# Routed experts of an attention + MoE kernel: second choices written plainly to first-choice slots, then added once into the output

## Time and profile before

| | value |
|---|---|
| median of three runs | 1812.68 us |
| the profiled execution | 1811.71 us, its span 1809.8 us |
| mean granted TensorE clock | 0.932 of full speed |
| PE / DVE / ACT / POOL busy | 82% / 69% / 43% / 71% of the span |
| chunk loop | from about 94 to 1196 us |
| first and last add into `out` (L466) | 1246.0 us and 1801.3 us; 288 instructions |

### The profile page before, as it was taken

One profiled execution on the slowest core, in us unless ns is written; L12 is line 12 of the kernel. 1 busy time (PEld: TensorE's weight loads), 2 busy tenths in 40 slices (PEclk: granted clock), 3 DMA queues, 4 the chain that ended last, 5 costly groups with the idle time before them and its releaser, 6 DMA issues.

```text
span 1809.8 us, 49252 instructions
## 1 busy us (share of the span) xinstructions
PE 1490.7 (82%) x17109; PEld 1315.5 (73%) x17110; DVE 1250.5 (69%) x3232; ACT 774.2 (43%) x1490; POOL 1276.1 (71%) x975
## 2 busy tenths in 40 slices
PE   5499999999999999999999999979776676676660
PEld 4477888888888888888888887758666665666650
DVE  7588888888888788888888887876434444334440
ACT  3244445445444444454455444425433333333330
POOL 5266666767676667666766766557888888888887
PEclk9699999999999999999999999999888889888885
DMA  8788888999898889888989988738777776777773
GB/s 195 136 212 184 171 174 209 197 178 192 209 183 179 192 194 188 180 192 211 180 174 210 201 174 185 178 137 213 136 130 134 134 133 108 132 132 134 134 113 36
DMA packets 929510, 302.36 MB, mean 167 GB/s; under 512 B 820882, under 2 KB 891160, under 8 KB 924480
## 3 DMA queue, kind: packets, MB, share of 16 engines
q1 hardware_dynamic: 859920, 178.50, 51.3%
q0 software_dynamic: 54432, 71.81, 21.7%
q10 hardware_dynamic: 15120, 51.57, 8.3%
HBM read 162.62 MB, written 143.43 MB: 169 GB/s over the span
## 4 chain that ended last, share of the span: by engine, by line
PE 38%; POOL 22%; issue 17%; DVE 14%; ACT 4%; SPq 2%; DMA 2%; POOLq 1%; DVEq 0%; ACTq 0%
POOL out L466 18%; ACT xn L568 3%; PE bank_a L1134 3%; PE bank_z L1119 3%; PE bank_y L1119 3%; PE bank_y L1121 3%; PE bank_y L1120 3%; PE bank_a L1273 3%; PE bank_z L1121 3%; PE bank_z L1120 3%; DVE ln_stats L879 2%; PE bank_a L1119 2%; PE bank_a L1121 2%; PE bank_a L1120 2%; PE bank_u L1119 2%
## 5 line engine op out<-in xcount | busy, mean ns | idle before, releaser
L466 POOL DMA_INDIRECT out<-v_area,tail x288 | 467.4, 1623 | 94.4 <-issue 89.1
L369 POOL DMA_INDIRECT slots<-xn,slot_i x256 | 263.8, 1031 | 134.5 <-DVE xn L830 71.7
L1119 PE MATMUL bank_y<-w_hi,xn_hi 128*128 x288 | 100.6, 349 | 148.8 <-DVE v_area L1075 81.7
L670 ACT ACTIVATE v_area<-bank_y,tail 128x256 f32<-128x256 f32 x144 | 60.5, 471 | 318.0 <-DVE tail L1067 314.1
L391 POOL TENSOR_TENSOR hid_lo<-hid,hid_hi 128x512 fp32r<-128x512 f32 x128 | 173.4, 1365 | 25.1 <-ACT hid_hi L539 23.6
L1119 PEld LDWEIGHTS bank_y<-w_hi,xn_hi 128*128 128x128 f32 x288 | 65.5, 228 | 163.9 <-issue 163.9
L1067 DVE COPY tail<-k_area 128x8 f32<-128x8 f32 x72 | 12.6, 175 | 245.7 <-DMA out<-v_area,tail 245.7
L539 ACT ACTIVATE hid_hi<-hid 128x512 fp32r<-128x512 f32 x128 | 80.6, 630 | 210.5 <-DVE hid L845 141.4
L1119 PE MATMUL bank_y<-wsh_out_hi,hid_hi 128*128 128x256 f32 x512 | 142.2, 278 | 0.0
L1120 PE MATMUL bank_y<-wsh_out_lo,hid_hi 128*128 128x256 f32 x512 | 141.9, 277 | 0.0
L1121 PE MATMUL bank_y<-wsh_out_hi,hid_lo 128*128 128x256 f32 x512 | 141.8, 277 | 0.0
(11 more groups left out here) (217 smaller groups left out, 4987.5 us busy)
## 6 DMA issues: line engine op xcount, KB each, us to landing
k_area<-slots SPq DMA_DIRECT2D x288, 129.0 KB
kv_dram<-w_sb SPq DMA_DIRECT2D x32, 1024.0 KB
x_sb<-in_x_in SPq DMA_DIRECT2D x32, 512.0 KB, 5.1
ctx_sb<-in_ctx_t SPq DMA_DIRECT2D x32, 512.0 KB, 5.0
q_dram<-q_sb SPq DMA_DIRECT2D x32, 512.0 KB
k_area<-kv_dram SPq DMA_DIRECT2D x256, 64.0 KB
w_sb<-q_dram SPq DMA_DIRECT2D x256, 64.0 KB
v_area<-kv_dram SPq DMA_DIRECT2D x256, 64.0 KB, 5.3
```

The lines of the kernel that those rows point to most:

```text
L369: pool.indirect_dma_start(slots[j], bass.IndirectOffsetOnAxis(ap=slot_i[:, j, i:i + 1], axis=0), row_of[j][:, i, :], None).then_inc(S[f"sc ...
L466: pool.indirect_dma_start(out, bass.IndirectOffsetOnAxis(ap=tail[:, r, t, 1 - j:2 - j].bitcast(u32), axis=0), y_ring[:, r, t, :], None, bo ...
L670: st = nc.scalar.activation(y_ring[:, r, t, :], Y[0][:, t * C:(t + 1) * C], ACT.Copy, scale=tail[:, r, t, j:j + 1])
L1119: mm(out, lhs_hi, rhs_hi, start=start, stop=False)
```

## The change

The roles are exchanged: the variable `FIRST = 1` names the table of the tokens' second choices, which is worked on in quads 0 to 35, and `SECOND = 0` that of the first choices, quads 36 to 71. Below, "first half" is quads 0 to 35 and "second half" quads 36 to 71.

- A row of a second choice no longer carries the token's number, but the row of the same token in the first choices' table (`SLOT_0`). In the first half POOL writes the weighted expert rows there, into a new table `sums`, with a plain indirect DMA (`ALU.bypass`). In the second half SP loads, beside the tiles, four tiles of `sums` into `y_ring` (`load_sums`), `expert_y` adds them, and POOL adds the result into `out`. Each token's row of `out` is thus added to once instead of twice.
- `expert_y` is DVE's alone, for all four tiles, and tells POOL after each two (`y_ready`). PE waits for both before its next `expert_down`.
- `pads(0)` also pads `sums` (six DMAs instead of three), comes before POOL's half of the `w2_lo` split instead of after it, and DVE waits for these pads before its half, since `pad` now lies where `y_ring` does.
- In the chunk loop the four steps of the shared block have four places (`hid_of`; two of them in `x_ring_t`), so that `shared_u` waits only for the chunk before. `x_round` and `x_split` of a chunk come one stage earlier (ACT between the copies of the turned tiles and their rounding, POOL ahead of `xn2_split`), `base_sum` writes to a buffer of its own, the scatters are in another order and their indices have two buffers.

```diff
+FIRST, SECOND = 1, 0
...
+        sums = nc.dram_tensor("sums", [NO_TILE + P, C], f32).ap()
...
-        pad = v_flat[:, 5632:5632 + PAD * ROW].rearrange("p (s f) -> p s f", s=PAD)
+        base = v_flat[:, 5120:5120 + BPC * C].rearrange("p (i f) -> p i f", i=BPC)
+        hid_of = [hid[:, 0, :], hid[:, 1, :]] + [x_ring_t[:, 2 * s:2 * s + 2, :].rearrange("p t f -> p (t f)") for s in range(2)]
+        pad_flat = v_flat[:, 0:PAD * ROW]
+        pad = pad_flat.rearrange("p (s f) -> p s f", s=PAD)
...
+            def load_x(j, n, r, at_rows, first):
+                if not first:
...
+                    sp.wait_ge(S["tail_ready"], at(1, n - 4, 1))
...
+                for t in range(4):
+                    sp.dma_start(x_ring[:, r, t, :], slots[j][bass.ds(at_rows[t], P), :]).then_inc(S[f"loaded{r}"], 16)
...
+            def load_sums(n, r, at_rows, first):
+                if not first:
+                    sp.wait_ge(S[f"added{r}"], at(16, n - r, 0))
+                for t in range(4):
+                    sp.dma_start(y_ring[:, r, t, :], sums[bass.ds(at_rows[t], P), :]).then_inc(S[f"held{r}"], 16)
...
+            sp.wait_ge(S["no_tile_stored"], 16 * (TOP + 1))
+            sp.wait_ge(S["padded1"], 16 * 3)
+            sp.wait_ge(S["scattered1"], 16 * BPC * CHUNKS)
+            first_rows = [tile_rows(q, q) for q in range(4)]
             for q in range(4):
-                load_quad(0, q, q, True, row_regs)
+                load_x(FIRST, q, q, first_rows[q], True)
             with sp.Fori(4, QUADS - 3, 4) as q:
                 for r in range(4):
-                    load_quad(0, q + r, r, False, row_regs)
...
+                    at_rows = tile_rows(q + r, r)
+                    load_x(FIRST, q + r, r, at_rows, False)
+            sp.wait_ge(S["scattered0"], 16 * BPC * CHUNKS)
+            sp.wait_ge(S["padded0"], 2 * 16 * 3)
+            second_rows = [tile_rows(QUADS + r, r) for r in range(4)]
+            for r in range(4):
+                load_x(SECOND, QUADS + r, r, second_rows[r], False)
+            for r in range(4):
+                sp.wait_ge(S[f"added{r}"], 16 * QUADS)
+            for r in range(4):
+                load_sums(QUADS + r, r, second_rows[r], True)
+            with sp.Fori(QUADS + 4, TOP * QUADS - 3, 4) as q:
                 for r in range(4):
-                    load_quad(1, q + r, r, False, row_regs)
+                    at_rows = tile_rows(q + r, r)
+                    load_x(SECOND, q + r, r, at_rows, False)
+                    load_sums(q + r, r, at_rows, False)
...
+            SCATTERS = [(j, i) for j in (FIRST, SECOND) for i in range(BPC)]
...
-                    nc.gpsimd.tensor_tensor(hid_lo[:, s, :], hid[:, s % 2, :], hid_hi[:, s, :], ALU.subtract).then_inc(S["hid_split"], 1)
+                    nc.gpsimd.tensor_tensor(hid_lo[:, s, :], hid_of[s], hid_hi[:, s, :], ALU.subtract).then_inc(S["hid_split"], 1)
...
+            def body(c, par, ahead_2):
                 xn2_split(c - 1)
-                if ahead:
-                    x_split(c + 1)
                 scale_probs(c)
-                scatter(c - 1, SCATTERS[:5])
-                hid_split(c - 1, range(2))
-                scatter(c - 1, SCATTERS[5:6])
+                scatter(c - 1, 1 - par, SCATTERS[:4])
+                hid_split(c - 1, range(1))
+                scatter(c - 1, 1 - par, SCATTERS[4:5])
+                hid_split(c - 1, range(1, 2))
+                scatter(c - 1, 1 - par, SCATTERS[5:6])
                 hid_split(c - 1, range(2, 3))
-                scatter(c - 1, SCATTERS[6:])
+                scatter(c - 1, 1 - par, SCATTERS[6:])
                 hid_split(c - 1, range(3, SB))
                 ln2_power(c)
                 if ahead_2:
                     ln1_power(c + 2, False)
                     ctx_split(c + 2)
-            with pool.Fori(1, CHUNKS - 2) as c:
-                body(c, True, True)
-            body(CHUNKS - 2, True, False)
-            body(CHUNKS - 1, False, False)
+                    x_split(c + 2)
...
+                for rows, width in ((slots[j], ROW), (sums, C))[:1 if j == FIRST else 2]:
+                    blocks = rows.rearrange("(b s) f -> b (s f)", s=PAD)
+                    for g in range(3):
+                        pool.indirect_dma_start(blocks if g else rows,
+                                                bass.IndirectOffsetOnAxis(ap=pad_at_i[:, j * 3 + g:j * 3 + g + 1], axis=0),
+                                                pad_flat[:, 0:PAD * width] if g else pad_flat[:, 0:width], None,
+                                                bounds_check=(NO_TILE + P) // (PAD if g else 1) - 1, oob_is_err=False).then_inc(S[f"padded{j}"], 16)
...
             xn2_split(CHUNKS - 1)
-            scatter(CHUNKS - 1, SCATTERS[:BPC])
+            scatter(CHUNKS - 1, 1, SCATTERS[:BPC])
             hid_split(CHUNKS - 1, range(1))
             pool.wait_ge(S["pad_at_ready"], 1)
             pool.wait_ge(S["pad_ready"], 1)
+            pads(1)
+            hid_split(CHUNKS - 1, range(1, SB))
+            scatter(CHUNKS - 1, 1, SCATTERS[BPC:])
             pads(0)
-            hid_split(CHUNKS - 1, range(1, SB))
-            scatter(CHUNKS - 1, SCATTERS[BPC:])
             pool.wait_ge(S["w2_hi_ready"], 1)
             pool.wait_ge(S["u_full"], SB * CHUNKS)
             half = slice(0, E * C // 2)
             nc.gpsimd.tensor_tensor(w2_lo[:, half], w2_sb[:, half], w2_hi[:, half], ALU.subtract).then_inc(S["w2_split"], 1)
-            pads(1)
-            def add(j, q, r):
-                n = j * QUADS + q
-                pool.wait_ge(S["ey_act"], at(1, n, 1))
-                pool.wait_ge(S["ey_dve"], at(1, n, 1))
-                pool.sem_inc(S["add_marked"], 1)
+            def pass_on(n, j, r):
+                target, last = (out, TOKENS - 1) if j == SECOND else (sums, NO_TILE + P - 1)
                 for t in range(4):
-                    pool.indirect_dma_start(out, bass.IndirectOffsetOnAxis(ap=tail[:, r, t, 1 - j:2 - j].bitcast(u32), axis=0),
-                                            y_ring[:, r, t, :], None, bounds_check=TOKENS - 1, oob_is_err=False,
-                                            compute_op=ALU.add).then_inc(S[f"added{r}"], 16)
-            pool.wait_ge(S["base_stored"], 16 * CHUNKS)
-            for q in range(4):
-                add(0, q, q)
-            with pool.Fori(4, QUADS - 3, 4) as q:
-                for r in range(4):
-                    add(0, q + r, r)
-            for r in range(4):
-                pool.wait_ge(S[f"added{r}"], 16 * QUADS)
+                    if t % 2 == 0:
+                        pool.wait_ge(S["y_ready"], at(2, n, t // 2 + 1))
+                        pool.sem_inc(S["add_marked"], 1)
+                    pool.indirect_dma_start(target, bass.IndirectOffsetOnAxis(ap=tail[:, r, t, 1 - j:2 - j].bitcast(u32), axis=0),
+                                            y_ring[:, r, t, :], None, bounds_check=last, oob_is_err=False,
+                                            compute_op=ALU.add if j == SECOND else ALU.bypass).then_inc(S[f"added{r}"], 16)
             with pool.Fori(0, QUADS - 3, 4) as q:
                 for r in range(4):
-                    add(1, q + r, r)
+                    pass_on(q + r, FIRST, r)
+            pool.wait_ge(S["base_stored"], 16 * CHUNKS)
+            with pool.Fori(QUADS, TOP * QUADS - 3, 4) as q:
+                for r in range(4):
+                    pass_on(q + r, SECOND, r)
...
-            def turned_out(c):
+            def turned_out(c, ahead_2):
                 for k in range(KT):
                     act.wait_ge(S["t2_full"], at(KT, c, k + 1))
                     nc.scalar.activation(xn2_t[:, k, :], XN2T_BANKS[k][:, :], ACT.Copy).then_inc(S["t2_out"], 1)
+                if ahead_2:
+                    x_round(c + 2)
...
-                    act.wait_ge(S["hid_split"], at(SB, c - 1, SB))
+                    act.wait_ge(S["hid_split"], at(SB, c - 1, 2))
                     load_x_t(c + 2)
...
-            def expert_y(n, j, r, first):
-                act.wait_ge(S["ey_full"], at(2, n, 1))
-                act.wait_ge(S["tail_ready"], at(1, n, 1))
-                if not first:
-                    act.wait_ge(S[f"added{r}"], at(16, n - r, 0))
-                for t in range(2):
-                    st = nc.scalar.activation(y_ring[:, r, t, :], Y[0][:, t * C:(t + 1) * C], ACT.Copy, scale=tail[:, r, t, j:j + 1])
-                st.then_inc(S["ey_act"], 1)
...
-                for j in range(TOP):
-                    st = nc.vector.tensor_copy(xn2[:, :, (1, 2 + C)[j]].bitcast(u32), row_id[:, :])
-                st.then_inc(S["row_step"], 1)
...
+                nc.vector.tensor_tensor(xn2[:, :, SLOT_0].bitcast(u32), slot_up[:, 0:BPC], slot_back[:, 0:BPC], ALU.add)
...
-                if s >= 2:
-                    dve.wait_ge(S["hid_split"], at(SB, c, s - 1))
-                nc.vector.scalar_tensor_tensor(out=hid[:, s % 2, :], in0=th[:, s % 2, :], scalar=0.5,
```

(30 more changed lines are left out.)

145 lines of the change are left out of this document (64 added, 81 removed).

## The result

The changed kernel takes 1841.3 us (median of four, 1836.9 to 1848.0) against 1814.1 us for the kernel before, timed beside it: a ratio of 1.015, 95% interval 1.010 to 1.019. Forecast were 1743 us with a range of 1716 to 1780. The profiled execution took 1842.6 us with a span of 1840.8, 31.0 more than before's 1809.8. Three marks split it: the first indirect DMA of `y_ring`, the first one of the second half, and the end.

A forecast was written before the change was run, and what follows sets the result against it. PE was taken to bound the chunk loop and POOL's instruction stream the routed phase. 1811.7 - 79 (first half) + 4 (second) + 6 (between) + 13 (start) - 14 (chunk loop) = 1741.7, plus 1.0 to the median: 1743 us, range 1716 to 1780.

The forecast's parts named there:

- First half: -79 us: Quads 0 to 35 with plain writes: 5.5 instead of 7.69 us per quad, -79 us, bounds -97 and 0.
- with POOL this much faster, who is next? DVE: First half: with writes at 5.3 us per quad, DVE comes next at 4.98 us, just under POOL.
- The price of the write: First half: a plain indirect write costs POOL 1.03 us like a scatter, plus a 0.30 us gap.
- DVE's 4.98 us: First half: DVE's round of 4.10 us per quad plus 0.88 for the two further `expert_y` it takes over.
- DVE or a slow PE bounds the first half: Rival: DVE's gap grows when PE or ACT is late; 6.3 us per quad, +29 us, 1772 us; chance 0.13.
- the plain write costs as much as the add: Rival: first half stays at 7.69 us per quad, only the costs remain, 1822 us, slower; chance 0.04.
- Between the halves: +6: `load_sums(36)` waits for the last plain writes: POOL idle 8.5 instead of 2.23 us, +6 us, bounds +3 and +12.
- Second half: +4: Quads 36 to 71: DMA engines fill to 7.8 us per quad against POOL's 7.69, +4 us, bounds -2 and +60.
- The loop over SP: Second half: `load_x(n+1)` queued behind `load_sums(n)`; 20.7 us per three quads, 6.9 per quad, hidden by POOL's 7.69.
- the first rival: Second half falls behind POOL through full DMA engines or SP's loop: 8.7 us per quad, +32, 1775 us; chance 0.17.
- Start: +13: Start of routed phase: DVE's `w2_lo` split waits for the pads and starts 13 us later; bounds +8 and +18.
- Chunk loop: -14: Chunk loop: `shared_u` no longer waits for `hid_split` (26 waits, 23.2 us); -14 us, bounds -23 and 0.

The follow-up runs named there:

- e4_one_write: Changed kernel, but the first half writes only the last of each quad's four tiles and the second half loads second choices' rows instead of `sums`; 1735.6 us.
- e13_small_loads: Changed kernel, but first-half tile loads from the fifth quad on bring only 8 bytes per row instead of 1032; chip 12, 1762.8 us.
- e9_order_wait: Changed kernel with second-half tile loads of quad n+1 ahead of quad n's `sums` loads, and DVE's pad wait moved ahead of its first `expert_y`; 1817.6 us.
- e12_hid_two: e10_combined with the chunk loop's `hid` back to two buffers instead of four, with the waits of the kernel before; chip 12, 1760.1 us.
- e5_no_sums: Changed kernel without the second half's loads of `sums`, `expert_y` being a plain product; chip 4, 1814.6 us.
- e16_best_025: e10_combined with two `hid` buffers and a POOL filler of about 0.25 us after each quad's four writes; chip 3, 1803.3 us.
- e17_best_065: e10_combined with two `hid` buffers and a POOL filler of about 0.65 us after each quad's four writes; chip 3, 1787.8 us.
- e18_pause_100: e12_hid_two with the POOL filler after each quad's four writes cut to about 1.0 us; chip 3, 1762.6 us.
- e8_quad_pause: Changed kernel with one POOL filler of about 1.3 us after each first-half quad's four plain writes; chip 0, 1803.5 us.
- e7_pace_short: Changed kernel with a POOL filler of about 0.25 us after every plain write of the first half; chip 0, 1808.8 us.
- e19_plain_pause: e12_hid_two with 40 semaphore increments on POOL's queue, touching no SBUF, instead of the subtraction after each quad's four writes; chip 12, 1737.8 us.
- e10_combined: Changed kernel with the edits of e8_quad_pause and e9_order_wait together; chip 12, 1768.5 us.

## Why the prediction was wrong

- **First half: -79 us became -4.** The step that failed is "with POOL this much faster, who is next? DVE". It took the slowest engine's work for the time of a quad and put the news between engines at nothing. The price of the write (1.01) was right, DVE's 4.98 us were an upper price (e4_one_write ran at 4.62), and where nothing is held the half runs as forecast: e13_small_loads took 5.35 us per quad with all the writes, forecast 5.5. What was missing is that rows of plain writes 1.3 us apart hold PE's results, for up to 8.06 us here. The trace of before couldn't show it: its adds are 1.9 us apart, and its rows of plain DMAs, the four scatters, are short. The prediction looked at every busy time, but not whether such a row had ever run beside a chain of short waits. It is partly a matter of the chip: e13_small_loads, on chip 12, took 1762.8 us in all, inside the range forecast, and what the changed kernel would take there is open. The rival "DVE or a slow PE bounds the first half" has the sign, not the cause or the size; "the plain write costs as much as the add" has the time and the wrong mechanism. PE's clock goes with it: 0.87 in the window of the changed kernel, 1.00 in those of e4_one_write and e13_small_loads, where PE is busy 137 and 131 of 150 us instead of 95.
- **Between the halves: +6, measured +4.9** (idle 7.07 instead of 2.23). Right.
- **Second half: +4 became +16.** The loop over SP was named, and the order on SP that makes it. Mis-sized was its length, 20.7 us for three quads against POOL's 23.1. It bound after all: 8.17 us per quad are 24.5 for three. e9_order_wait shows it, since taking `load_x(n+1)` out of the loop gives the half back. The loop was added up from transfers measured with half as many loads, which is the likely reason; its parts were not measured again. This is the first rival, at 0.5 instead of 1.0 us per quad. The 2.3 us for a tile that the prediction set beside its 5.5 are, on the page that it names, a figure for DMAs issued by GpSimd, and these loads are SP's; the sum didn't use them.
- **Start: +13, measured +14.1.** Right in size and in the wait: DVE's split began at 1248.21, behind the pads. But only 7.24 us of DVE's idle time are put down to them, since `base_sum` had been held until 1239.68, another 11.68 us idle ahead of it. In e13_small_loads, where it wasn't held, DVE waited 17.48 us for the pads and the first write came no earlier (32.6 us after the last scatter). Only 4 us came back when the wait moved, because held results or late tile loads take its place.
- **Chunk loop: -14 became 0.** DVE's wait of 23 us was taken for a gain of PE. It did vanish, and the chunk loop took 1111 us as before. By e12_hid_two the four buffers cost 8 us instead of giving 14, and with them `ctx_lo` is slower and PE waits longer for it; so the rest of the change, costed at nothing, must have given about as much. Which part of it did is not shown. The Trainium skill (SBUF — State Buffer, section "Who interferes with whom") says that a DVE instruction with two SBUF inputs contends with a GpSimd instruction that reads SBUF; `ctx_lo` at 1439 and 1322 ns is in keeping with it, though no run separates this cause from others. The prediction applied that section to `expert_y` only, where nothing speaks against it: a write took 1.01 us in the changed kernel, with the scatter's price of 1.03 forecast.
- **The signs** named in the prediction did separate the cases: two groups of DMAs at 1.01 and 1.57 us (right), the split waiting for the pads (right), no DVE wait for `hid_lo` in the chunk loop (right). Of the signs against it, POOL waiting for DVE in the second half came, 24.3 us in 200; but "a first half in which POOL has gaps" was asked only together with "DVE has none". Both had gaps, and that was in no rival.

## What to carry to other kernels

When a bound engine is made faster, its instructions come in long rows that the trace of before never shows; before trusting the next bound, look for such a row beside the same neighbours. When nothing in a window is full, look at the distance from the end of a matmul to the start of what needs it, and at what another engine does in just that time. And behind an in-order queue, put what the next step needs ahead of what waits for the last one. When experiments run on several chips, run the kernel with the fault beside each of them, and compare first a stretch that no edit touches: here that stretch shows that five of eighteen experiments ran where the fault doesn't occur.

## What the runs showed of the hardware

- On chips 0, 3 and 4 plain indirect DMAs of 128 rows from POOL, 1.3 us apart in rows of up to eleven, with tile loads from SP beside them, hold the news of PE's matmuls for up to 10.6 us (e5_no_sums); it mostly comes 0.8 to 1.8 us after the last DMA of the row. A break of 0.6 us (e16_best_025) or 0.9 us (e17_best_065) after four writes doesn't end it, one of 1.2 us (e18_pause_100) or 1.5 us (e8_quad_pause) does but for 2.4 us, and so does a break of 0.6 us after every write (e7_pace_short). With one write per quad or with adds 1.9 us apart it did not show.
- On chip 12 it did not show in any of five kernels, not in the row of ten nor in sixteen writes in one row (e19_plain_pause). What sets that chip apart is open, and so is whether the tile loads take part.
- The Trainium skill (SBUF — State Buffer, section "Who interferes with whom") has PE and ACT wait for nobody; that is said of SBUF's ports, and here PE's results came late with no wait on a port to show for it. Through which path they are held stays open.
- POOL's subtraction stretched four DVE copies from 0.9 to 2.65 us (e10_combined). By the same section the engine that issues first has the shared ports for its whole instruction; the rows agree.
